# A graph-attention and quantised feed-forward kernel: quantised rows behind Wo written as int8 by ScalarE and widened by one VectorE copy, and two of eight output blocks scaled by VectorE

## The reference

```
x = x + gnn(_layernorm(x))                  # ... @ wo.T + bo
y = _layernorm(x)
def _act_fake_quant(x, clip_factor):
    scale = sigmoid(clip_factor) * max(abs(x)) / 127.0      # one scale for the whole array
    return clip(round(x / scale), -128.0, 127.0) * scale
xq   = _act_fake_quant(y, clip_x)
gate = xq @ weight_fake_quant(w_gate).T     # 352 x 1024, one scale for each row
up   = xq @ weight_fake_quant(w_up).T       # 352 x 1024
h    = _act_fake_quant(silu(gate) * up, clip_down)          # 384 x 352
x    = x + h @ weight_fake_quant(w_down).T  # 1024 x 352
```

## Time and profile before

| | before |
|---|---|
| time, median of 3 runs | 338.96 us |
| lowest and highest run | 338.02 and 339.05 us |
| span of the profiled execution, first to last instruction | 335.6 us |
| PE busy | 323.4 us (96%) |
| DVE busy | 236.5 us (70%) |
| ACT busy | 183.3 us (55%) |
| granted TensorE clock, mean | 1.000 |

### The profile page before, as it was taken

How to read it: one execution, slowest core, us unless ns; L and a number is a source line. 1 busy time by engine, 2 the same in 40 slices (tenths; PEclk the granted TensorE clock), 3 DMA queues, 4 the chain that set the end, 5 groups by cost and what they waited for, 6 DMA issues and landing times.

```text
span 335.6 us, 6006 instructions
## 1 busy us (share of the span) xinstructions
PE 323.4 (96%) x2086; PEld 297.1 (89%) x2086; DVE 236.5 (70%) x613; ACT 183.3 (55%) x335; POOL 187.4 (56%) x250
## 2 busy tenths in 40 slices
PE   5999999999999999999799999999999999999984
PEld 5899998878999999999799999999999878887854
DVE  4857887954075554449985978879797875597864
ACT  4824258372843333333265968678595865243573
POOL 6886667456787667479946393563726757000000
PEclk9999999999999999999999999999999999999999
DMA  7997346567044434653232141303213120000005
GB/s 255 376 396 275 125 127 178 201 227 239 17 127 149 128 109 154 235 191 113 76 125 65 63 126 63 127 10 118 66 60 127 63 65 0 0 2 0 2 0 187
DMA packets 17371, 41.70 MB, mean 124 GB/s; under 512 B 3537, under 2 KB 8001, under 8 KB 17345
## 3 DMA queue, kind: packets, MB, share of 16 engines
q1 hardware_dynamic: 14432, 38.87, 34.0%
q0 software_dynamic: 2064, 1.80, 1.8%
q10 hardware_dynamic: 848, 0.70, 0.6%
HBM read 37.99 MB, written 3.37 MB: 123 GB/s over the span
## 4 chain that ended last, share of the span: by engine, by line
PE 84%; DVE 9%; ACT 2%; issue 1%; DMA 1%; POOL 1%; DVEq 0%; ACTq 0%
PE PS L744 60%; PE PS L901 5%; PE PS L889 5%; PE PS L877 4%; DVE scratch L1294 2%; PE PS L1036 2%; DVE scratch L1293 1%; PE PS L725 1%; DMA X<-in_x 1%; PE PS L1090 1%; PE PS L813 1%; PE PS L803 1%; PE PS L788 1%; PE PS L735 1%; PE PS L807 1%
## 5 line engine op out<-in xcount | busy, mean ns | idle before, releaser
L414 POOL TENSOR_TENSOR ring<-stage,ring 128x256 fp32r<-128x256 f32 x124 | 95.5, 804 | 40.6 <-ACT ring L497 39.4
L744 PE MATMUL PS<-XT,ring 128*128 128x384 f32 x528 | 93.6, 336 | 0.5 <-DVE QT L1196 0.5
L744 PEld LDWEIGHTS PS<-XT,ring 128*128 128x128 f32 x528 | 91.4, 188 | 0.9 <-issue 0.8
L431 POOL DMA_INDIRECT codes<-ecol,place x51 | 57.0, 1118 | 27.8 <-DMA codes<-ecol,place 15.2
L497 ACT ACTIVATE ring<-stage 128x1024 fp32r<-128x1024 f32 x52 | 54.3, 1057 | 7.1 <-issue 3.7
L602 ACT ACTIVATE scratch<-scratch,smx 128x384 f32<-128x384 f32 x48 | 28.9, 604 | 21.0 <-DVE smx L1316 21.0
L1234 DVE TENSOR_TENSOR ring<-stage,ring 128x1024 fp32r<-128x1024 f32 x21 | 25.6, 1225 | 16.6 <-ACT ring L497 16.6
L744 PE MATMUL PS<-QT,ring 128*128 128x384 f32 x192 | 35.6, 339 | 1.5 <-DVE Q L1303 1.5
L744 PE MATMUL PS<-AT,ring 128*128 128x384 f32 x192 | 35.2, 338 | 0.0
L744 PEld LDWEIGHTS PS<-QT,ring 128*128 128x128 f32 x192 | 33.1, 188 | 2.1 <-issue 2.1
L744 PEld LDWEIGHTS PS<-AT,ring 128*128 128x128 f32 x192 | 33.0, 188 | 1.5 <-issue 1.5
(11 more groups left out here) (201 smaller groups left out, 477.8 us busy)
## 6 DMA issues: line engine op xcount, KB each, us to landing
stage<-in_weights SPq DMA_DIRECT2D x56, 512.0 KB
V<-in_w_gate_up SPq DMA_DIRECT2D x4, 512.0 KB
scratch<-codes POOLq DMA_DIRECT2D x3, 576.0 KB, 6.9
X<-in_x SPq DMA_DIRECT2D x3, 512.0 KB, 5.0
out<-X SPq DMA_DIRECT2D x4, 384.0 KB, 2.6
codes<-scratch SPq DMA_DIRECT2D x2, 576.0 KB, 13.3
scratch<-in_w_gate_up SPq DMA_DIRECT2D x2, 512.0 KB
V<-in_w_down SPq DMA_DIRECT2D x5, 176.0 KB
```

Source lines behind the costliest of these rows:

```text
L414: ins = pool.tensor_tensor(ring[1][:, slot, piece], stage[:, slot % STAGE, piece], ring[0][:, slot, piece].bitcast(F32), ALU.subtract)
L431: pool.indirect_dma_start(codes[b].rearrange("(n a) -> n a", a=1), bass.IndirectOffsetOnAxis(ap=place[:, t:t + 1], axis=0), ecol[:, VAL, t ...
L744: ins = pe.matmul(outs, lhs[a], rhs[b], start=start and n == 0, stop=stop and n == 2, skip_group_check=True)
```

## The change

ScalarE's copies of the six turned units, and of blocks 1 and 2 of `hid`, write int8 in place of float32. VectorE's two steps on each become one copy from int8 to bfloat16 (`widen`). Block 0 of `hid`, which VectorE does alone, goes from three steps to two: a product written as int8, and the same copy. The factors of the second product (`wsc`) are made three units earlier in VectorE's order. Output blocks 1 and 3 are scaled by VectorE, with a semaphore of their own, and ScalarE scales the other six. One wait that stands twice in TensorE's loop is left out once.

```diff
+BY_ACT, BY_DVE = (0, 2, 4, 5, 6, 7), (1, 3)
+        unit_q = [unit[:, 0, :].bitcast(I8).rearrange("p (k n) -> p k n", k=4) for unit in units]
+        hid_q = [V2[:, i, C - P:C - P + N // 4].bitcast(I8) for i in range(IT)]
...
-                act.activation(units[0][:, ks, :], turned(0, 0)[:, ks, :], ACT.Copy, scale=gmx[:, 11:12]
+                act.activation(unit_q[0][:, ks, :], turned(0, 0)[:, ks, :], ACT.Copy, scale=gmx[:, 11:12]
...
-                act.activation(units[u], turned(hf, m), ACT.Copy, scale=gmx[:, 11:12]).then_inc(t_ready, 1)
+                act.activation(unit_q[u], turned(hf, m), ACT.Copy, scale=gmx[:, 11:12]).then_inc(t_ready, 1)
...
-                act.activation(hid[0:iw, i, :], hid[0:iw, i, :], ACT.Copy,
+                act.activation(hid_q[i][0:iw, :], hid[0:iw, i, :], ACT.Copy,
...
-            for j in range(KT):
+            for j in BY_ACT:
                 act.wait_ge(d_full, j + 1)
                 act.activation(down_t[j], PS[:, DOWN[0][j % 4], 0:N], ACT.Copy, scale=dsc[:, j:j + 1]).then_inc(d_scaled, 1)
...
+            def scaled(j):
+                if j in BY_DVE:
+                    pe.wait_ge(d_scaled_v, BY_DVE.index(j) + 1)
+                else:
+                    pe.wait_ge(d_scaled, BY_ACT.index(j) + 1)
...
             for j in range(4, KT):
-                pe.wait_ge(d_scaled, j - 3)
                 turn_back(j - 4)
...
-            def round_off(src, dst):
-
-                chain.step(dve.tensor_scalar(src, src, QMAX, -QMAX - 1.0, ALU.min, ALU.max))
-                return dve.tensor_scalar(dst, src, MAGIC, MAGIC, ALU.add, ALU.subtract)
+            def widen(src, dst):
+
+                return dve.tensor_copy(dst, src)
...
-            chain.step(dve.tensor_scalar(hid[:, 0, :], hid[:, 0, :], gmx[:, 12:13], QMAX, ALU.mult, ALU.min))
-            chain.step(dve.tensor_scalar(hid[:, 0, :], hid[:, 0, :], -QMAX - 1.0, MAGIC, ALU.max, ALU.add))
-            dve.tensor_scalar(hq[:, 0, :], hid[:, 0, :], MAGIC, None, ALU.subtract).then_inc(hq_ready, 1)
+            chain.step(dve.tensor_scalar(hid_q[0], hid[:, 0, :], gmx[:, 12:13], None, ALU.mult))
+            widen(hid_q[0], hq[:, 0, :]).then_inc(hq_ready, 1)
...
+            dve.wait_ge(dsc_ready, 1)
+            for j in BY_DVE:
+                dve.wait_ge(d_full, j + 1)
+                dve.tensor_scalar(down_t[j], PS[:, DOWN[0][j % 4], 0:N], dsc[:, j:j + 1], None, ALU.mult
+                                  ).then_inc(d_scaled_v, 1)
```

More of the change, by code:

```diff
@@ L20 @@
 I32 = mybir.dt.int32
+I8 = mybir.dt.int8
 ALU = mybir.AluOpType
@@ L262, in gnn_ffn @@
         d_scaled = sem("d_scaled")
+        d_scaled_v = sem("d_scaled_v")
         back_full = sem("back_full")
@@ L1093, in down @@
                         ins.then_inc(d_full, 1)
+            def scaled(j):
[3 more added lines that the diff above has]
+                    pe.wait_ge(d_scaled, BY_ACT.index(j) + 1)
             def turn_back(j):
-                pe.wait_ge(d_scaled, j + 1)
+                scaled(j)
                 if j >= 4:
@@ L1465, in _ @@
                 dve.wait_ge(t_ready, part + 1)
-                round_off(units[0][:, ks, :], xqT[:, ks, 0:P]).then_inc(xq_ready, 1)
+                widen(unit_q[0][:, ks, :], xqT[:, ks, 0:P]).then_inc(xq_ready, 1)
             for u in range(1, 2 * NT):
@@ L1469, in _ @@
                 dve.wait_ge(t_ready, u + 2)
[L1470 to L1473, removed]
+                widen(unit_q[u], xqT[:, 4 * hf:4 * hf + 4, m * P:(m + 1) * P]).then_inc(xq_ready, 1)
+                if u == NT:
+                    dve.wait_ge(x_scaled, 1)
+                    dve.tensor_scalar(wsc[:, :, :], fsc[:, 1, :, 0].rearrange("p (g i) -> p g i", g=2), gmx[:, 9:10],
+                                      clip[:, 2, 0:1], ALU.mult, ALU.mult).then_inc(scales_ready, 1)
             for i, (_, iw) in enumerate(I_TILES):
@@ L1491, in _ @@
             dve.wait_ge(h_scale, 1)
-            chain.step(dve.tensor_scalar(hid[:, 0, :], hid[:, 0, :], gmx[:, 12:13], QMAX, ALU.mult, ALU.min))
-            chain.step(dve.tensor_scalar(hid[:, 0, :], hid[:, 0, :], -QMAX - 1.0, MAGIC, ALU.max, ALU.add))
-            dve.tensor_scalar(hq[:, 0, :], hid[:, 0, :], MAGIC, None, ALU.subtract).then_inc(hq_ready, 1)
+            chain.step(dve.tensor_scalar(hid_q[0], hid[:, 0, :], gmx[:, 12:13], None, ALU.mult))
+            widen(hid_q[0], hq[:, 0, :]).then_inc(hq_ready, 1)
             for i, (_, iw) in enumerate(I_TILES[1:], 1):
                 dve.wait_ge(ht_ready, i)
-                round_off(hid[0:iw, i, :], hq[0:iw, i, :]).then_inc(hq_ready, 1)
+                widen(hid_q[i][0:iw, :], hq[0:iw, i, :]).then_inc(hq_ready, 1)
+            dve.wait_ge(dsc_ready, 1)
[3 more added lines that the diff above has]
+                                  ).then_inc(d_scaled_v, 1)
             for j in range(KT):
```

## The result

| | before | changed |
|---|---|---|
| median of 20 runs | 338.77 us | 337.81 us |
| lowest and highest | 337.99 and 340.5 us | 337.09 and 339.76 us |
| ratio, 95% interval | | 0.9966 (0.9952 to 0.998) |

What follows compares the result with a forecast made beforehand. TensorE, busy 96% of the span, was taken to bound the kernel, so removed VectorE time pays only where TensorE waits. 0.2 + 0.29 + 0 = 0.49 us, from 338.96 to 338.5 us, range 337.8 to 339.3.

Steps and rivals of the forecast that it cites:

- The two stalls: TensorE's waits for quantised pieces at the gate and up input and the down input, shortened by 0.2 and 0.29 us.
- the rival of a restart set by TensorE itself: Down input: TensorE's restart behind its constants, not VectorE, sets the 0.49 us idle; only 0.2 gained, 338.75 us; chance 0.12.
- The wait for ScalarE's second whole unit: Second up block: TensorE waits for ScalarE's unit copy, leaving about 0.2 of the 0.32 us gained at the gate input.
- Byte operands: the fast bound: VectorE's int8 steps at the down input run as fast as float32 rows, gaining 0.29 us; slow bound 0.07.
- The rival with one element per cycle: Byte operands run at one element per cycle on VectorE; gain 0.27 us in all, 338.7 us; chance 0.17.
- a slower ScalarE: ScalarE writes bytes at half its pace, delaying units and hidden blocks; net +0.9 us, 339.9 us; chance 0.07.
- The two blocks by VectorE: Output scaling: VectorE takes blocks 1 and 3 at 0.5 to 0.55 us each; costs 0 and gains 0.
- The double wait costs nothing: TensorE's turn-back loop: the wait that stands twice was priced at 0 us.
- the 0.61 us that I had taken for the largest gain possible: Both stalls together: the most they allow, 0.32 + 0.29 us, less than 1.0 us.
- Launch and end, untouched by the change: Outside the span: the 3.4 us from span to median is launch and end and stays the same.
- Faster by over 0.3%: Whole kernel: an outcome held to come only from the spread of the measurement; chance 0.13.

Runs made afterwards that it cites:

- e10: The changed kernel with nine in place of eleven constant products ahead of the down product; stretch 20.11 us against 20.21.
- e11: The changed kernel with fifteen in place of eleven constant products ahead of the down product; stretch 20.86 us against 20.21.
- e5: The changed kernel with all eight output blocks scaled by ScalarE again, double wait still out; stretch 20.22 us, ratio 0.9961 to the kernel before.
- e6: The kernel before with only the double wait taken out of TensorE's loop; median 338.32 us against 338.97, ratio 0.9994, stretch 20.75 us.
- e13: The changed kernel with the double wait of TensorE's loop put back; median 338.55 us, ratio 0.9989 to the kernel before, stretch 20.27 us.
- e15: The kernel before with only the double wait taken out, run again; median 338.18 us, ratio 0.9982, stretch 20.75 us.
- e16: The kernel before, unchanged, run once more; median 339.32 us, ratio 1.0016, stretch 20.81 us.

## Why the prediction was wrong, and what of it held

**The two stalls: right in mechanism and size.** 0.2 and 0.29 were forecast, 0.24 and 0.29 measured, 0.25 and 0.32 in the kernels with one part each. The constants do end last at the down input (`e10`, `e11`), and the restart behind them follows the cast, so the rival of a restart set by TensorE itself fell. The wait for ScalarE's second whole unit took 0.09 us off the 0.32 where I had taken 0.12.

**Byte operands: the fast bound.** A copy from int8 to bfloat16 takes what the float32 row of the same size took. By the Trainium skill (VectorE: DVE Perf Modes, What auto-detection actually checks) a one-source op with both operands in SBUF gets two elements per cycle whatever its type. The trace agrees: 0.43 for 512 columns and 0.66 for two of 256, as with float32, where 512 columns took 0.43 and 256 took 0.30 and 0.29. The rival with one element per cycle fell, and so did that of a slower ScalarE.

**The two blocks by VectorE: worth nothing,** as forecast (`e5`, 20.22 against 20.21). Each took about 0.6 rather than 0.5 to 0.55, and the first add followed at once.

**"The double wait costs nothing": the step that failed.** I had put this term at 0 without a reason. It costs 0.10 us of the chain where TensorE stands waiting at it, which happens once, and that is the missing tenth of the stage. With it fell the 0.61 us that I had taken for the largest gain possible: the interval begins at 0.7. More weighs what I had no eye for: with those four waits left out the last instruction fetch lies in another place. With them in, it fell into the output transfers in five of eight profiles, the slowest landing came 0.8 to 1.6 us late, and the tail grew from 5.15 to between 5.31 and 6.79 us in four of them.

**"Launch and end, untouched by the change": wrong as well.** Of the 3.4 us between the span and the median, 2.1 lie outside the span, and 1.1 to 1.3 are by how much the profiled execution happened to be short. Its fetch fell behind the output, so its tail was a short one (5.14), and I took it for the kernel's own. The median starts from 338.77 over 20 runs, not 338.96. That 337.81 still falls into my range, by a hundredth, is luck: the range was widened for the spread of the runs and for nothing else.

**The account.** 0.62 us is shown in the stage, part by part. The fetch's place, the late landing and the longer tail where it falls into the output are shown by profiles. That this makes up the rest of the 1.15 us is argued: the estimate of 0.46 us from the tails has the right size, and the medians of `e6`, `e13`, `e15` and the counts go the right way, but the size is within the noise of the ratios. Why four waits move the fetch, and why its place varies by execution when they are in, was not tried.

**The chances.** "Faster by over 0.3%" had 0.13, because I let nothing but the spread of the measurement carry it. The interval (0.2% to 0.48%) does not settle on which side of 0.3% the kernel lies. If it lies above, an edit that I had costed at nothing carried it there.

## What to carry to other kernels

Take two profiles and compare stretches, never spans: here one stretch repeated to 0.02 us in four profiles of the kernel before, while spans of one kernel differed by over 1 us. Give each removed instruction a price, a wait that repeats another included, and look at what runs besides the work at the end, instruction fetches among it, before calling the end fixed. Work taken from an engine pays only where another stands still for it: VectorE is busy 2.2 us less in the stretch (13.3 in place of 15.5), and the two stalls gave back 0.53 us.

## What was not expected of the hardware

- A second wait for the same value of the same semaphore, right behind the first, delays TensorE by 0.10 us where it stood waiting (0.14 against 0.04 us from the end of ScalarE's copy, in 8 and in 12 profiles).
- One instruction fetch of 0.02 MB among output transfers of four times 384 KB goes with 3.6 to 4.4 us in place of 2.8 for the slowest landing (five profiles against fifteen), and with up to 1.6 us more at the end. In `e16` the last packets of the output go through at the pace of one DMA engine in sixteen.
- As forecast, but in no row before: ScalarE writes int8 at the pace of float32, 0.84 us for two copies of 256 columns from PSUM in both kernels.
